# Ready-made byte addresses for the moving windows of a counting stage on one Trainium2 core

## The chip, the cores and the metric

One core of a Trainium2 chip runs the whole program. The metric is the device time of one execution in microseconds (us); the kernel before takes 1166.79 us (median of 3 runs, 1166.59 to 1166.88). PE is the matrix engine and PEld its weight load, DVE the vector engine, ACT the scalar engine, POOL the GpSimd engine, SP the engine that issues DMAs. Each engine has a sequencer, which reads the instructions in order, runs register and load instructions itself and hands the others to the engine.

## The reference, cut to what matters

The reference is a network of four graph layers on 3125 nodes and 100,000 edges, whose `dst` is sorted. The layers are an attention layer, a layer with an edge softmax over each destination, a summing layer, and one with three Chebyshev filters. The sums over edges have one form:

```
def _segment_sum(src, seg, n): return jax.ops.segment_sum(src, seg, n)
h_e = jax.ops.segment_sum(h[src], dst, num_segments=h.shape[0])      # layer 3
def prop(h): return segment_sum(wn[:, None] * h[row], col, n)          # layer 4
```

The kernel doesn't gather rows per edge. Its first stage, the count stage, builds a dense table `CT[source, destination]`: how many edges run from each source to each destination. All later sums over edges are matrix products with `CT`. This stage is the one that the change touches.

## The kernel before, in words

**The stages.** The program is one block with a stream of instructions per engine. `build_*` is the count stage, then come `proj_*`, `attn_*`, `prop_*` and `last_*`; between the first stages stands a meeting (`meet`, L71) at which all five engines wait for each other. The count stage ends at its first meeting, at about 360 us.

**How edges become counts.** The sorted edges are cut into chunks of 128. An item is one chunk against one window of four destinations (W = 4). Five items (GI = 5) that follow each other along the destinations make a group, four groups make a set (20 items), and six sets make a block of 120. There are 313 groups in 80 sets, and 14 blocks. Even groups walk the first half of the items, odd groups the second half, so group g and group g-2 touch neighbouring or equal places of `CT`, and g and g-1 do not.

**Per block.** POOL fetches the block's edges with two indirect DMAs (`gather`, L202 and L205) and makes keys of them (`keys`, L212 to L224). DVE splits the source number (`high`, L444 and L447), TensorE turns the keys (`turn_items`, L520 and L522), and ACT copies them out (`keep_items`, L576).

**Per set, on DVE.** Two large comparisons (both L435) make one-hot matrices: `oneS`, 128 edges by 20 items by 128 low source digits, and `mov`, 128 edges by 20 items by 100 columns (25 high source digits by 4 destinations). Each has two buffers (DEEP = 2). DVE may write the buffer of set s once TensorE has finished set s-2 (semaphore `counted`). Between the sets DVE runs the pieces of the edge softmax in an order written out by hand (`SOFT_AT`), and small jobs (`high`, `passes`, `slots`, `table`).

**Per set, on TensorE.** `load_windows` (L478 to L490) waits for the table and reads the set's 20 words from SBUF into registers: one TENSOR_LOAD, L485. Then come four groups. A group is five matmuls of 100 columns into one PSUM bank (L551), each shifted by its window's start, and one matmul with the identity (L555) that adds what `CT` holds at the group's place, 500 columns. Before L555 the stream waits until group g-2 has been placed back (semaphore `placed`). ACT waits for `counted` and writes the 500 sums into `CT` (L589), which adds one to `placed`.

**Where the addresses come from.** TensorE computes the first destination of each window into PSUM (`windows`, L513): a group's first word holds the start, the other four the distance from it (matrix `turnW`). DVE converts them to whole numbers in `wI` (`table`, L414), in item order. A table word is thus an offset in elements. `bass.ds(value, n)` turns it into an address: a register instruction (FUSED_REGOPS in the trace) multiplies the word by the element size and adds the base address. There is one before each of the 1252 shifted matmuls of L551 (the first of a group isn't shifted), one before each of the 313 matmuls of L555, and one before each of the 313 placements of L589. Where a semaphore wait stands before such an instruction, it is carried out on the register instruction: that of `placed` on the one of L555, that of `counted` on the one of L589. ACT reads every fifth word of the set, four in all.

Of the kernel before, what the change touches and what calls it, by code (L numbers as in the profile page):

```python
# [4 lines left out]
F32 = mybir.dt.float32  # L5
# [4 lines left out]
ALU = mybir.AluOpType  # L10
# [12 lines left out]
W = 4  # L23
WS = 2
LH = 795
NW = NP // W
# [22 lines left out]
class Kern:  # L49
# [15 lines left out]
    def sb(self, st, name, shape, dt):  # L65
        return st.enter_context(self.nc.sbuf_tensor(name, shape, dt))
# [34 lines left out]
GI = 5  # L101
SETS = 80
SET = 4 * GI
BLOCK = 6 * SET
# [16 lines left out]
             25: (4, 1)}  # L121


def before(g):

    return sum(1 for p in PRESENT if p < g)


def alloc_build(K, st):
    sb = K.sb  # L130
    K.iotaM = sb(st, "iotaM", [128, 25 * W], I16)
    K.iotaX = sb(st, "iotaX", [128, 128], I16)

    K.KL = sb(st, "KL", [128, RING, 2, BLOCK, 2], I16)
    K.GS = sb(st, "GS", [128, 2, CH], I32)
    K.GD = sb(st, "GD", [128, 2, CH], I32)
    K.dl = sb(st, "dl", [128, CH], F32)
    K.over = sb(st, "over", [128, CH], F32)
    K.under = sb(st, "under", [128, CH], F32)
    K.hi = sb(st, "hi", [128, 2, CH], I32)  # L140
    K.key = sb(st, "key", [128, CH], F32)
    K.va = sb(st, "va", [128, CH], F32)
    K.lo = sb(st, "lo", [128, 2, CH], F32)
    K.wI = [sb(st, "wI%d" % h, [b - a, BLOCK], I32) for h, (a, b) in enumerate(PARTS)]
    K.turnW = sb(st, "turnW", [BLOCK, BLOCK], F32)
    K.win = sb(st, "win", [BLOCK, NJ], F32)
    K.cI = sb(st, "cI", [BLOCK, NJ], I32)
    K.i4 = sb(st, "i4", [BLOCK, NJ], F32)
    K.jI = sb(st, "jI", [BLOCK, NJ], I32)
    K.row0 = sb(st, "row0", [1, BLOCK], F32)  # L150
    K.col0 = sb(st, "col0", [BLOCK, 1], F32)
    K.zf = sb(st, "zf", [128, 1], F32)
    K.onef = sb(st, "onef", [1, 1], F32)
    K.oneh = sb(st, "oneh", [128, 1], F16)
    K.lw = sb(st, "lw", [128, 7], I32)
    K.le = sb(st, "le", [128, 7], F32)
    K.cc = sb(st, "cc", [128, 7], I32)
    K.oneS = sb(st, "oneS", [128, DEEP, SET, 128], F16)
    K.mov = sb(st, "mov", [128, DEEP, SET, 25 * W], F16)
    K.cs = sb(st, "cs", [128, 4], F32)  # L160

    with ExitStack() as st2:
        K.iotaS = sb(st2, "iotaS", [128, SLOTS], I16)
        K.past = sb(st2, "past", [128, 7, 7 * BLOCK], F16)
    K.wv = sb(st, "wv", [128, J], F32)
    K.sp = sb(st, "sp", [128, J], BF16)
    K.sn = sb(st, "sn", [128, J], BF16)
    K.A1 = sb(st, "A1", [128, J], F32)
    K.A2 = sb(st, "A2", [128, J], F32)
    K.A3 = sb(st, "A3", [128, J], F32)  # L170
    K.ie = sb(st, "ie", [128, J], BF16)
    K.rows = sb(st, "rows", [1, 400], F32)
    K.CTf = K.CT[:, :, :].rearrange("p a d -> p (a d)").bitcast(F32)
# [196 lines left out]
def build_vector(v, K):  # L370
# [2 lines left out]
    v.memset(K.lw[:, 6:7], 32000).then_inc(S("lw_set"), 1)  # L373
    v.memset(K.zf[:, :], 0.0).then_inc(S("zf"), 1)
    v.memset(K.onef[:, :], 1.0)
    v.memset(K.oneh[:, :], 1.0).then_inc(step, own.up())


# [31 lines left out]

    def table(h):

        v.wait_ge(S("windows"), h + 1)
        v.tensor_copy(K.wI[h][:, :], K.bank(4)[0:PARTS[h][1] - PARTS[h][0], 128:128 + BLOCK]).then_inc(S("reg_set"), 1)  # L414

    for t in range(7):
        passes(0, t)
    v.wait_ge(S("identf"), 1)
    ident = K.identf[0:BLOCK, 0:BLOCK]
    v.tensor_copy(K.turnW[:, :], ident).then_inc(step, own.up())  # L420
    first = ident[:, 0:BLOCK:GI].unsqueeze(2).to_broadcast([BLOCK, BLOCK // GI, GI - 1])
    v.wait_ge(step, own.n)
    v.tensor_tensor(K.turnW[:, :].rearrange("p (m k) -> p m k", k=GI)[:, :, 1:GI],
                    ident.rearrange("p (m k) -> p m k", k=GI)[:, :, 1:GI], first, ALU.subtract).then_inc(step, own.up())
    slots(0)
    v.wait_ge(S("iota"), 6)
    v.wait_ge(S("passed"), 1)
# [48 lines left out]
    v.wait_ge(step, own.n)  # L476


def load_windows(K, e, ety, s, every):

    j, o = s // 6, SET * (s % 6)
    h = 0 if j == 0 else 1 if j < PARTS[2][0] else 2
    r = j - PARTS[h][0]
    e.wait_ge(K.S("reg_set"), h + 1)
    _, vals = K.nc.values_load_multi_w_load_instructions(  # L485
        K.wI[h][r:r + 1, o:o + SET:every], engines=[ety], min_val=0, max_val=W * (NW - 3),
        skip_runtime_bounds_check_because="a window's first destination by the staircase")
    n = SET // 4 // every
    return [[x if k == 0 else x.with_bounds(min_val=0, max_val=(GI - 1) * W) for k, x in enumerate(vals[n * r:n * r + n])]
            for r in range(4)]  # L490


def build_tensor(t, K):
    S, bank = K.S, K.bank
    t.wait_ge(K.own["v"].sem, K.row0_at)
    t.matmul(bank(5)[0:BLOCK, 0:1], K.row0[:, :], K.onef[:, :], start=True, stop=True).then_inc(S("item0"), 1)

    def sums(h):
        a, b = PARTS[h]
        for j in range(a, b):  # L500
            for t_ in range(7):
                if j == a:
                    t.wait_ge(S("past"), 7 * h + t_ + 1)
                m = t.matmul(bank(4)[0:BLOCK, j:j + 1], K.past[:, t_, BLOCK * (j - a):BLOCK * (j - a + 1)], K.oneh[:, :],
                             start=(t_ == 0), stop=(t_ == 6))
        m.then_inc(S("passed"), 1)

    def windows(h):
        a, b = PARTS[h]
        t.wait_ge(S("slot_w"), h + 1)  # L510
        if h:
            t.wait_ge(S("reg_set"), h)
        t.matmul(bank(4)[0:b - a, 128:128 + BLOCK], K.win[:, a:b], K.turnW[:, :], start=True, stop=True  # L513
                 ).then_inc(S("windows"), 1)

    def turn_items(j):
        t.wait_ge(S("key"), j + 1)
        if j:
            t.wait_ge(S("items"), j)
        t.transpose(bank(6)[:, 0:BLOCK], K.va[0:BLOCK, :], K.identf[0:BLOCK, 0:BLOCK])  # L520
        t.wait_ge(S("lo"), j + 1)
        t.transpose(bank(6)[:, BLOCK:2 * BLOCK], K.lo[0:BLOCK, j % 2, :], K.identf[0:BLOCK, 0:BLOCK]  # L522
                    ).then_inc(S("key_turned"), 1)

    def soft_turn(n, back):
        t.wait_ge(S("scan_v"), 2 * n + back + 1)
        if not back:
            t.transpose(bank(7)[0:1, 0:128], K.cs[:, 0:1], K.identf[:, :])
            t.transpose(bank(7)[0:1, 128:256], K.cs[:, 1:2], K.identf[:, :]).then_inc(S("scan_p"), 1)
        else:  # L530
            src = K.rows[:, 257:385] if n in (1, 3) else K.rows[:, 256:384]
            t.transpose(bank(7)[:, 256:257], src, K.identf[0:1, 0:1]).then_inc(S("scan_p"), 1)

    sums(0)
    windows(0)
    sums(1)
    turn_items(0)
    windows(1)
    t.wait_ge(S("identb"), 1)
    t.wait_ge(S("zero"), 5)  # L540
    for g in PRESENT:
        s, o = g // 4, GI * (g % 4)
        if g % 4 == 0:
            words = vals = to = None
            words = load_windows(K, t, mybir.EngineType.PE, s, 1)
            t.wait_ge(S("one_hot"), s + 1)
        vals = words[g % 4]
        ps = bank(g % 4)[:, 0:25 * GI * W].rearrange("p (a c) -> p a c", a=25)
        for k in range(GI):
            to = ps[:, :, 0:W] if k == 0 else ps[:, :, bass.ds(vals[k], W)]  # L550
            t.matmul(to, K.oneS[:, s % DEEP, o + k, :], K.mov[:, s % DEEP, o + k, :].rearrange("p (a w) -> p a w", a=25),  # L551
                     start=(k == 0), stop=False, skip_group_check=True)
        if g >= 2:
            t.wait_ge(S("placed"), INDEX[g - 2] + 1)
        t.matmul(ps, K.identb[:, :], K.CT[:, :, bass.ds(vals[0], GI * W)], start=False, stop=True, skip_group_check=True  # L555
                 ).then_inc(S("counted"), 1)
        if g == PRESENT[-1] or g // 4 != PRESENT[INDEX[g] + 1] // 4:
            if s == SUM_AT:
                sums(2)
            if s == SLOTS_AT:  # L560
                windows(2)
            if s in TURN_AT:
                turn_items(TURN_AT[s])
            if SOFT_AT.get(s) in SOFT_TURN:
                soft_turn(*SOFT_TURN[SOFT_AT[s]])
    t.wait_ge(S("counted"), len(PRESENT))


def build_scalar(a, K):
    S = K.S  # L570
# [13 lines left out]
    for i, g in enumerate(PRESENT):  # L584
        s = g // 4
        if g % 4 == 0:
            words = load_windows(K, a, mybir.EngineType.Activation, s, GI)
        a.wait_ge(S("counted"), i + 1)
        a.activation(K.CT[:, :, bass.ds(words[g % 4][0], GI * W)],  # L589
                     K.bank(g % 4)[:, 0:25 * GI * W].rearrange("p (a c) -> p a c", a=25), ACT.Copy).then_inc(S("placed"), 1)  # L590
        if g == PRESENT[-1] or s != PRESENT[i + 1] // 4:
            if s in TURN_AT:
# [1458 lines left out]
```

## Time and profile before

| | |
|---|---|
| median of 3 runs | 1166.79 us |
| span of the profiled execution, first to last instruction | 1161.5 us |
| what lies around the span, against that median | 5.3 us |
| busy share of the span: PE, DVE, ACT, POOL | 86%, 75%, 52%, 42% |
| mean granted TensorE clock over the span | 0.934 |
| the count stage | 0 to 360 us |

The profile is of one execution of its own; no separate time is given for it, so its span and the median are set side by side. Times in the trace are microseconds from the first instruction, durations are nanoseconds where it says so. A row of a group of instructions gives the line in the kernel, engine, operation, output<-input, count, busy time, the mean of one, and the engine's idle time before them with what ended it. "issue" means that nothing which the profile shows ended the wait: the sequencer itself was late. Register instructions and loads into registers belong to the sequencer; they are not counted as busy and carry the mark "q" behind the engine.

### The profile page before, as it was taken

The page shows a single profiled execution, that of the slowest core. Times are in us where ns is not written, and L with a number is a line of the kernel's source. Part 1 is how long each engine was busy: PE and PEld are TensorE (multiplying, and loading weights), DVE is VectorE, ACT ScalarE, POOL GpSimd, SP SyncE. Part 2 cuts the span into 40 slices and gives each one's busy share as a digit, 9 for nine tenths or more (in the row PEclk, how much of TensorE's full clock was granted, in tenths as well). Part 3 has the DMA queues.
Part 4 walks back from the last instruction along what each step waited for, and adds up shares of the span by engine and source line. Part 5 has one row for each costly group of instructions (what it writes and reads, how often), then busy time and mean ns, then how long its engine had stood idle before and what let it go on. Part 6 is the DMA issues. An engine that isn't in the chain of part 4 may idle for free.

```text
span 1161.5 us, 23065 instructions
## 1 busy us (share of the span) xinstructions
PE 1003.2 (86%) x8302; PEld 612.5 (53%) x8302; DVE 876.5 (75%) x1318; ACT 608.1 (52%) x824; POOL 492.1 (42%) x522
## 2 busy tenths in 40 slices
PE   3887777777778779999999999996999699999995
PEld 2554455554544423223223333333669599999984
DVE  8668888888765569999999999997846654543366
ACT  7455556565563579898989898881100000001132
POOL 8434443343310069999999999980000000000000
PEclk9788999896897979999999999997999799999997
DMA  0010000000001631222222223221001100010111
GB/s 9 25 44 8 10 6 5 6 5 8 17 1 50 202 82 44 62 50 63 48 59 51 64 58 72 51 65 48 1 1 42 42 25 24 2 35 11 57 45 42
DMA packets 98715, 44.63 MB, mean 38 GB/s; under 512 B 85006, under 2 KB 96526, under 8 KB 98482
## 3 DMA queue, kind: packets, MB, share of 16 engines
q1 hardware_dynamic: 96914, 41.43, 13.4%
q0 software_dynamic: 1696, 1.74, 0.6%
q8 instruction: 73, 1.20, 0.4%
q14 instruction: 32, 0.26, 0.1%
HBM read 30.58 MB, written 12.56 MB: 37 GB/s over the span
## 4 chain that ended last, share of the span: by engine, by line
PE 77%; issue 9%; DVE 7%; ACT 3%; DMA 1%; POOL 1%; SPq 1%; DVEq 0%; ACTq 0%; POOLq 0%
PE PS L1298 18%; PE PS L1062 12%; PE PS L551 11%; PE PS L1072 11%; PE PS L555 8%; PE PS L1306 3%; PE PS L1773 3%; PE PS L1051 3%; ACT Eb L1114 2%; PE PS L1289 1%; POOL Eb L975 1%; DVE Eb L1134 1%; PE PS L875 1%; DMA kd<-QH 1%; PE PS L1759 1%
## 5 line engine op out<-in xcount | busy, mean ns | idle before, releaser
L1114 ACT ACTIVATE Eb<-PS,small 128x1024 f32<-128x1024 f32 (+4 forms) x350 | 333.3, 1003 | 45.0 <-PE PS L1062 40.3
L1134 DVE TENSOR_TENSOR Eb<-Eb,PS 128x2048 f32<-128x2048 f32 (+4 forms) x175 | 341.8, 2011 | 18.8 <-POOL Eb L975 10.1
L975 POOL TENSOR_SCALAR Eb<-Eb 128x1024 f32<-128x1024 f32 (+4 forms) x350 | 318.9, 935 | 76.7 <-ACT Eb L1114 73.2
L589 ACT ACTIVATE CT<-PS 128x500 f32 x313 | 183.7, 587 | 142.5 <-PE PS L555 134.3
L551 PE MATMUL PS<-mov,oneS 128*128 128x100 f16 x1565 | 183.3, 228 | 78.8 <-issue 74.7
L551 PEld LDWEIGHTS PS<-mov,oneS 128*128 128x128 f16 x1565 | 145.4, 105 | 158.4 <-issue 112.6
L1298 PE MATMUL PS<-hs,CT 128*128 128x192 f16 (+1 forms) x2500 | 213.3, 247 | 3.6 <-DVE SG L1539 1.6
L1298 PEld LDWEIGHTS PS<-hs,CT 128*128 128x128 f16 (+1 forms) x2500 | 207.9, 99 | 7.3 <-DVE SG L1539 2.3
L1062 PE MATMUL PS<-Qb,Kb 96*128 96x512 f16 (+3 forms) x700 | 180.4, 362 | 13.7 <-DMA Kb<-kd 10.8
L435 DVE TENSOR_TENSOR oneS<-iotaX,KL 128x2560 f16<-128x2560 int16 x80 | 120.4, 1505 | 70.3 <-PE PS L555 67.8
L1072 PE MATMUL PS<-Eb,V 128*25 128x512 f32 (+3 forms) x1400 | 166.7, 548 | 0.8 <-DVE Eb L1134 0.8
L1062 PEld LDWEIGHTS PS<-Qb,Kb 96*128 96x128 f16 (+1 forms) x700 | 42.3, 98 | 198.6 <-ACT Eb L1114 184.4
L555 PE MATMUL PS<-CT,identb 128*128 x313 | 139.1, 444 | 1.0 <-ACT CT L589 0.8
L1739 POOL MEMSET CT<- 1x384 f32 x1 | 0.4, 416 | 305.9 <-PE PS L1298 305.9
L435 DVE TENSOR_TENSOR mov<-iotaM,KL 128x2000 f16<-128x2000 int16 x80 | 98.7, 1234 | 0.0
L217 POOL TENSOR_SCALAR key<-hi 120x128 f32<-120x128 int32 x14 | 8.8, 628 | 172.9 <-DVE hi L444 172.9
L1419 ACT ACTIVATE hs<-PS 96x96 f32<-96x96 f32 x9 | 2.2, 247 | 138.2 <-PE PS L1330 138.2
L1051 PEld LDWEIGHTS PS<-identb,CT 128*128 128x128 f16 (+1 forms) x625 | 49.5, 98 | 44.0 <-DVE Eb L1134 7.8
L1051 PE MATMUL PS<-identb,CT 128*128 128x128 f16 (+1 forms) x625 | 66.5, 220 | 4.4 <-DVE Eb L1134 4.4
L1539 DVE TENSOR_REDUCE SG<-PS 128x96 f32<-128x192 f32 (+1 forms) x75 | 24.8, 352 | 60.1 <-PE PS L1298 59.8
L1773 PE MATMUL PS<-hs,CT 97*128 97x297 f32 (+1 forms) x200 | 42.8, 357 | 0.3 <-ACT CT L1820 0.3
L1306 PE MATMUL PS<-CT,identb 128*128 128x500 f16 (+1 forms) x157 | 38.2, 400 | 3.3 <-SPq L71 3.3
(281 smaller groups left out, 905.9 us busy)
## 6 DMA issues: line engine op xcount, KB each, us to landing
Kb<-kd SPq DMA_DIRECT2D x168, 96.0 KB, 2.3
qd<-QH SPq DMA_DIRECT2D x12, 192.0 KB, 2.7
kd<-QH SPq DMA_DIRECT2D x12, 192.0 KB, 3.1
hs<-t_d SPq DMA_DIRECT2D x12, 192.0 KB, 2.5
Qb<-qd SPq DMA_DIRECT2D x4, 384.0 KB, 3.8
CT<-x_d SPq DMA_DIRECT2D x1, 1200.0 KB, 7.1
x_d<-B SPq DMA_DIRECT2D x6, 192.0 KB, 1.9
t_d<-A SPq DMA_DIRECT2D x6, 192.0 KB, 1.8
```

The source lines that it names most:

```text
L435: return v.tensor_tensor(out.rearrange("p e (c two) -> p e c two", two=2), v_in, k_in, ALU.is_equal)
L551: t.matmul(to, K.oneS[:, s % DEEP, o + k, :], K.mov[:, s % DEEP, o + k, :].rearrange("p (a w) -> p a w", a=25), start=(k == 0), stop=False ...
L555: t.matmul(ps, K.identb[:, :], K.CT[:, :, bass.ds(vals[0], GI * W)], start=False, stop=True, skip_group_check=True).then_inc(S("counted"), 1)
L589: a.activation(K.CT[:, :, bass.ds(words[g % 4][0], GI * W)], K.bank(g % 4)[:, 0:25 * GI * W].rearrange("p (a c) -> p a c", a=25), ACT.Copy ...
L975: g.tensor_scalar(e, e, EHI, ELO, ALU.min, ALU.max).then_inc(S("clamped"), 1)
L1051: m = p.transpose(K.cntv[it % 2][0:r, 128 * i:128 * i + w], K.CT[0:w, B0[b] + i, 128 * t:128 * t + r], K.identb[0:w, 0:w])
L1062: m = p.matmul(bank(h)[0:r, 0:wb], K.Kb[:, it % NK, h, 0:r], K.Qb[:, b % 2, h, 0:wb], start=True, stop=True)
L1072: m = p.matmul(bank(4)[32 * h:32 * h + 25, 0:wb], K.V[0:r, t, h, :], K.Eb[0:r, it % NE_, h, 0:wb], start=(t == 0), stop=(t == NT - 1), til ...
L1114: a.activation(e, ps, ACT.Exp, scale=K.unsc[0:r, :]).then_inc(S("score_exp"), 1)
L1134: v.tensor_tensor(e, e, cn, ALU.mult).then_inc(S("weighed"), 1)
L1298: m = p.matmul(bank(t % FIRST)[0:r, 0:w], K.CT[:, a, 128 * t:128 * t + r], hs[:, a, :, :].rearrange("p k d -> p (k d)"), start=(a == 0), s ...
L1773: m = p.matmul(ps[:, c:297], K.TT[0:r, s, 128 * k:128 * k + 128], K.GC[0:r, k, c:297], start=(k == 0), stop=(k == 3), skip_group_check=True)
```

## The change

- The table holds byte addresses. Its 20 words of a set are in a new order: first the starts of the four groups, as addresses in `CT`, then four times four addresses in the PSUM bank of the group. `turnW` is scaled so that the products are bytes (by 2 for `CT`, by 4 for PSUM); `table` adds the base address of `CT` with one instruction and the banks' addresses (`bankA`, set by four memsets) with another.
- The expressions in `load_windows` take the base off again and divide by the element size, so that the address that the program asks for is the loaded word itself, with no register instruction in between.
- With no register instruction before L555 and L589, the waits for `placed` and `counted` stand on the matmul and on the placement.
- ACT reads four words that are neighbours, where it read every fifth of twenty. TensorE still reads twenty.

```
+    K.bankA = sb(st, "bankA", [7, 4], F32)
+    K.ct_at = K.nc.lookup_mloc(K.CT).addr
+    for q in range(4):
+        v.memset(K.bankA[:, q:q + 1], float(PSUM_AT + BANK_BYTES * q))
...
     def table(h):
+        n = PARTS[h][1] - PARTS[h][0]
         v.wait_ge(S("windows"), h + 1)
-        v.tensor_copy(K.wI[h][:, :], K.bank(4)[0:PARTS[h][1] - PARTS[h][0], 128:128 + BLOCK]).then_inc(S("reg_set"), 1)
+        ps = K.bank(4)[0:n, 128:128 + BLOCK].rearrange("r (s q k) -> r s q k", q=4, k=GI)
+        words = K.wI[h][:, :].rearrange("r (s w) -> r s w", w=SET)
+        v.tensor_scalar(words[:, :, 0:4], ps[:, :, :, 0], float(K.ct_at), None, ALU.add).then_inc(step, own.up())
+        banks = K.bankA[0:n, :].unsqueeze(1).unsqueeze(3).to_broadcast([n, BLOCK // SET, 4, GI - 1])
+        v.tensor_tensor(words[:, :, 4:SET].rearrange("r s (q k) -> r s q k", q=4), ps[:, :, :, 1:GI], banks, ALU.add
+                        ).then_inc(S("reg_set"), 1)
...
-    v.tensor_copy(K.turnW[:, :], ident).then_inc(step, own.up())
+    v.tensor_scalar(K.turnW[:, :], ident, 2.0, None, ALU.mult).then_inc(step, own.up())
...
+    v.wait_ge(step, own.n)
+    rest = K.turnW[:, :].rearrange("p (m k) -> p m k", k=GI)[:, :, 1:GI]
+    v.tensor_scalar(rest, rest, 4.0, None, ALU.mult).then_inc(step, own.up())
...
-def load_windows(K, e, ety, s, every):
+def load_windows(K, e, ety, s, rest):
...
     _, vals = K.nc.values_load_multi_w_load_instructions(
-        K.wI[h][r:r + 1, o:o + SET:every], engines=[ety], min_val=0, max_val=W * (NW - 3),
+        K.wI[h][r:r + 1, o:o + (SET if rest else 4)], engines=[ety], min_val=K.ct_at, max_val=PSUM_AT + 4 * BANK_BYTES,
...
+    starts = [(x.with_bounds(min_val=K.ct_at, max_val=top, guaranteed_mod_val=0, out_of_modulus=2) - K.ct_at) // 2
+              for x in vals[0:4]]
+    inside = [[(x.with_bounds(min_val=PSUM_AT + BANK_BYTES * q, max_val=PSUM_AT + BANK_BYTES * q + 4 * REL_MAX,
+                              guaranteed_mod_val=0, out_of_modulus=4) - PSUM_AT) // 4
+               for x in vals[4 + (GI - 1) * q:4 + (GI - 1) * (q + 1)]] for q in range(4 if rest else 0)]
...
-            to = ps[:, :, 0:W] if k == 0 else ps[:, :, bass.ds(vals[k], W)]
+            to = ps[:, :, 0:W] if k == 0 else bass.AP(K.PS, inside[g % 4][k - 1], [[4096, 128], [GI * W, 25], [1, W]])
...
-        t.matmul(ps, K.identb[:, :], K.CT[:, :, bass.ds(vals[0], GI * W)], start=False, stop=True, skip_group_check=True
+        t.matmul(ps, K.identb[:, :], K.CT[:, :, bass.ds(starts[g % 4], GI * W)], start=False, stop=True, skip_group_check=True
...
-        a.activation(K.CT[:, :, bass.ds(words[g % 4][0], GI * W)],
+        a.activation(K.CT[:, :, bass.ds(starts[g % 4], GI * W)],
```

## Rows read from the trace of the kernel before

**Rows 1.** The page's costliest groups, lines of the count stage.

```profile
L589 ACT ACTIVATE CT<-PS 128x500 f32 x313 | 183.7, 587 | 142.5 <-PE PS L555 134.3
L551 PE MATMUL PS<-mov,oneS 128*128 128x100 f16 x1565 | 183.3, 228 | 78.8 <-issue 74.7
L435 DVE TENSOR_TENSOR oneS<-iotaX,KL 128x2560 f16<-128x2560 int16 x80 | 120.4, 1505 | 70.3 <-PE PS L555 67.8
L435 DVE TENSOR_TENSOR mov<-iotaM,KL 128x2000 f16<-128x2000 int16 x80 | 98.7, 1234 | 0.0
```

**Rows 2.** Busy time of each engine from the first one-hot to the stage's end.

```profile
core 0: us, PE busy (x) PEld busy (x) DVE busy (x) ACT busy (x) POOL busy (x), PEclk, DMA share, GB/s
22.50:360.00 337.50, 256.78 (x1965) 166.11 (x1965) 262.86 (x249) 194.95 (x328) 128.11 (x117) 0.87 0.04 12
```

**Rows 3.** Timeline of PE over one set: start us, us, instructions, idle before.

```profile
202.02 0.68 PE L551 MATMUL PS<-mov,oneS 128*128 128x100 f16 x5 [1.06 <-issue]
202.60 0.39 PE L555 MATMUL PS<-CT,identb 128*128 x1
203.26 0.39 PE L555 MATMUL PS<-CT,identb 128*128 x1
...
204.52 0.39 PE L555 MATMUL PS<-CT,identb 128*128 x1
```

**Rows 4.** Sequencer instructions by source line, whole trace: min/median/max ns.

```profile
L485 PEldq TENSOR_LOAD <-wI x80: 1355/1359/1549, 29.3 to 356.7; - x80
L551 PEldq FUSED_REGOPS  x1252: 37/46/51, 30.9 to 358.5; - x179
L555 PEldq FUSED_REGOPS  x313: 37/42/42, 31.4 to 358.6; - x157
```

**Rows 5.** Timelines of ACT and DVE over the same set.

```profile
203.10 2.50 ACT L589 ACTIVATE CT<-PS 128x500 f32 x4 [1.43 <-PE PS L555]
201.07 1.49 DVE L435 TENSOR_TENSOR oneS<-iotaX,KL 128x2560 f16<-128x2560 int16 x1 [1.59 <-PE PS L555]
202.48 1.19 DVE L435 TENSOR_TENSOR mov<-iotaM,KL 128x2000 f16<-128x2000 int16 x1
```

**Rows 6.** Who waited for whom, 22.5 to 360 us: total us, times, longest.

```profile
POOL key L217 <- DVE hi L444: 172.9, 13, 18.2
DVE oneS L435 <- PE PS L555: 67.8, 56, 4.6
```

**Rows 7.** Timeline of PEld around the L555 matmul that starts at 202.60 us.

```profile
202.59 0.10 PEld L555 LDWEIGHTS PS<-CT,identb 128*128 128x128 f16 x1
202.61 0.10 PEld L551 LDWEIGHTS PS<-mov,oneS 128*128 128x128 f16 x1
```

**Rows 8.** Back-to-back 500-column matmuls at full clock, and five-matmul groups at half clock.

```profile
849.66 2.76 PE L1306 MATMUL PS<-CT,identb 128*128 128x500 f16 x12
...
47.92 0.62 PE L555 MATMUL PS<-CT,identb 128*128 x1
48.33 0.62 PE L551 MATMUL PS<-mov,oneS 128*128 128x100 f16 x5
48.76 0.62 PE L555 MATMUL PS<-CT,identb 128*128 x1
```

**Rows 9.** Third load of table words, and PE's timeline around it.

```profile
L485 PEldq TENSOR_LOAD <-wI x1: 1358/1358/1358, 44.9 to 44.9; - x1
...
42.54 4.31 PE L504 MATMUL PS<-oneh,past 128*120 128x1 f16 x42
```

**Rows 10.** DVE: the long wait near the start, the table, and `turnW`.

```profile
50.31 1.49 DVE L435 TENSOR_TENSOR oneS<-iotaX,KL 128x2560 f16<-128x2560 int16 x1 [4.60 <-PE PS L555]
L414 DVE CAST wI<-PS x3: 208/262/264, 22.4 to 61.2; 1x120 int32<-1x120 f32 x1, 7x120 int32<-7x120 f32 x1, 6x120 int32<-6x120 f32 x1
9.82 0.26 DVE L423 TENSOR_TENSOR turnW<-identf 120x96 f32<-120x96 f32 x1
```

More of the change, by code:

```diff
@@ L121 @@
              25: (4, 1)}
+PSUM_AT = 0x2000000
+BANK_BYTES = 2048
+REL_MAX = (GI - 1) * W
 def before(g):
@@ L484, in load_windows @@
     e.wait_ge(K.S("reg_set"), h + 1)
+    top = K.ct_at + 2 * W * (NW - 3)
     _, vals = K.nc.values_load_multi_w_load_instructions(
-        K.wI[h][r:r + 1, o:o + SET:every], engines=[ety], min_val=0, max_val=W * (NW - 3),
[L487 to L490, printed above, removed]
+        K.wI[h][r:r + 1, o:o + (SET if rest else 4)], engines=[ety], min_val=K.ct_at, max_val=PSUM_AT + 4 * BANK_BYTES,
+        skip_runtime_bounds_check_because="addresses made from a window's first destination by the staircase")
+    starts = [(x.with_bounds(min_val=K.ct_at, max_val=top, guaranteed_mod_val=0, out_of_modulus=2) - K.ct_at) // 2
[3 more added lines that the diff above has]
+               for x in vals[4 + (GI - 1) * q:4 + (GI - 1) * (q + 1)]] for q in range(4 if rest else 0)]
+    return starts, inside
 def build_tensor(t, K):
@@ L543, in build_tensor @@
         if g % 4 == 0:
-            words = vals = to = None
-            words = load_windows(K, t, mybir.EngineType.PE, s, 1)
+            starts = inside = to = None
+            starts, inside = load_windows(K, t, mybir.EngineType.PE, s, True)
             t.wait_ge(S("one_hot"), s + 1)
-        vals = words[g % 4]
         ps = bank(g % 4)[:, 0:25 * GI * W].rearrange("p (a c) -> p a c", a=25)
         for k in range(GI):
-            to = ps[:, :, 0:W] if k == 0 else ps[:, :, bass.ds(vals[k], W)]
+            to = ps[:, :, 0:W] if k == 0 else bass.AP(K.PS, inside[g % 4][k - 1], [[4096, 128], [GI * W, 25], [1, W]])
             t.matmul(to, K.oneS[:, s % DEEP, o + k, :], K.mov[:, s % DEEP, o + k, :].rearrange("p (a w) -> p a w", a=25),
@@ L586, in build_scalar @@
         if g % 4 == 0:
-            words = load_windows(K, a, mybir.EngineType.Activation, s, GI)
+            starts, _ = load_windows(K, a, mybir.EngineType.Activation, s, False)
         a.wait_ge(S("counted"), i + 1)
-        a.activation(K.CT[:, :, bass.ds(words[g % 4][0], GI * W)],
+        a.activation(K.CT[:, :, bass.ds(starts[g % 4], GI * W)],
                      K.bank(g % 4)[:, 0:25 * GI * W].rearrange("p (a c) -> p a c", a=25), ACT.Copy).then_inc(S("placed"), 1)
```

## The prediction

> **What bounds the kernel now.** I read the page's groups first [rows 1]. In the count stage DVE's two one-hot builds and ACT's placements wait for PE's L555, and PE's L551 waits for "issue", 74.7 us in all: the stage's pace comes from PE's sequencer. The window over the stage [rows 2] shows no engine full in its 337.5 us: DVE 262.9, PE 256.8 by modelled ends, ACT 195.0. The timeline of one set [rows 3] splits that. PE's L555 matmuls start at 202.60 and 203.26, and the fourth at 204.52, so a group takes (204.52 - 202.60) / 3 = 0.64 us. The array needs less: twelve 500-column matmuls back to back take 2.76 us, thus about 0.22 each, and at half clock five matmuls of 100 columns take 48.33 - 47.92 = 0.41 us including their share of the next [rows 8], so 0.21 at full clock. That makes 0.43 us a group. What fills 0.64 is the sequencer. By source line [rows 4], each shifted matmul has a register instruction of 46 ns median; the group shows 0.64 / 5 = 0.13 us for a register instruction, a weight load and a matmul. Then, once a set, the sequencer loads 20 words in 1.36 us [rows 4]. In this set nothing covers that: PE stood idle for 1.06 us before its next L551 at 202.02 [rows 3]. From the first L551 at 202.02 over the fourth L555 at 204.52 and the load to the next first L551 it is 2.50 + 1.36 + 0.05 = 3.9 us; 337.5 / 80 = 4.2 us with the start and the stretches at half clock. I take 4.05 for a set.
>
> **The change, part by part.**
>
> *Register instructions.* 1252 + 313 go from PE's sequencer, at 46 and 42 ns: 57.6 + 13.1 = 71 us of register work, and more with what stands around each. ACT loses 313. What is left to issue is a weight load and a matmul, and these come close together: the weight load of L555 at 202.59, its matmul (whose address is already in a register) at 202.60 [rows 3], the next weight load at 202.61 [rows 7]. So I cost a pair at 0.01 to 0.02 us, 24 pairs a set at 0.4 us. The other bound is that a register-addressed matmul without its register instruction costs what the whole step costs now, 0.13 us; no row speaks for that, the 0.01 us between neighbours speaks against it.
>
> *The waits move.* Today `placed` is waited for on the register instruction, so the sequencer stands there until ACT has placed group g-2 and only then goes on to the next group and to the table load. With the wait on the matmul the sequencer can hand it over and read on. What is queued behind the waiting instruction: the next group's five matmuls, which write another bank and need nothing of ACT, and then the next set's load. That a load runs while matmuls are still outstanding is shown once: the third TENSOR_LOAD starts at 44.9 us, while L504's 42 matmuls run from 42.54 to 46.85 [rows 9]; at 4.31 / 42 = 0.10 us each that leaves about 18 of them to come. So the sequencer may lead by some 17 matmuls, most of a set of 24, and a load of 1.36 us then hides behind the last three groups. The Trainium skill (Advanced Engine Details and Errata, Engine Queue Depths) gives TensorE a queue of 64 instructions, ScalarE 8. By it the lead would be 32 pairs, a whole set and more; by the row it is about 17 pairs; the load hides by either. No row shows a register-addressed matmul that itself carries a wait; that is the open point, bounded by 0 (it queues like others) and by the load's whole 1.36 us a set (the sequencer stands as before).
>
> *ACT.* Its placements run at 2.50 / 4 = 0.63 us [rows 5], 587 ns of it work [rows 1]. The round from L555 over ACT back to L555 of g+2 is 0.39 (matmul) + 0.11 (its end 202.99 to ACT's 203.10) + 0.59 + about 0.1 = 1.2 us for two groups, 0.6 a group. So on a set with full buffers PE and ACT need 4 x 0.61 = 2.44 us. ACT's four neighbouring words in place of four strided ones are at most its load, which its sequencer can now do ahead; I cost it at nothing, with ACT idle for 142.5 us as cover.
>
> *DVE becomes the bound.* A set's one-hots take from 201.07 to 203.67, 2.60 us [rows 5], over 2.44. Added up with the softmax pieces and the small jobs DVE has 262.9 us of work [rows 2]; it doesn't shrink. Of its idle 74.6 us, 67.8 are waits for PE's L555 [rows 6]. I keep 5 us of them: the longest, 4.60 us at 50.31 [rows 10], comes from the 42 matmuls of L504, which stay. After the last one-hot one group has to be counted and placed: 0.2 + 0.4 + 0.6 = 1.2 us, say 1.4.
>
> *What is added.* DVE gets one more table instruction for each of three tables and one more for `turnW`, 0.26 us each [rows 10], 1.0 us together on an engine that is now the bound; the four memsets lie in its wait for POOL at the start. The bounds are 0.3 us (only `turnW` late) and 2 us.
>
> *The clock.* The granted clock of the stage is 0.87 on average [rows 2]. It has two levels, 1.2 and 2.4 GHz, so about 26% of the stage, 88 us or some 21 sets, is at half. There a group is array-bound at 48.76 - 47.92 = 0.84 us [rows 8], a set 3.35. Today that hides under 4.05; against a DVE set of 2.60 it costs 0.75 us. With the softmax pieces a set of DVE is 262.9 / 80 = 3.3 on average, and about two thirds of the sets are well under that: 21 x 0.67 x 0.75 = 10.5 us if the share stays. PE will do the same matmuls in less time, with shorter pauses, so I expect fewer falls and take half, 5 us; bounds 0 and, with the whole stage at half clock, 80 x 3.35 = 268 plus some 30 us for the long softmax sets, 298, less the 269 us (262.9 + 5 + 1.4) without it: 29 us.
>
> **Sum.** 262.9 + 5 + 1.4 + 1.0 + 5 = 275.3 us in place of 337.5: 62 us less. The span goes from 1161.5 to 1099.3. The stages behind begin at a meeting of all engines, so they move forward as they are; the softmax's last output is written well before. The median of the runs shown stands 5.3 us above the profiled span (1166.8), so the time is 1104.6, rounded to 1105 us.
>
> **The rivals.**
>
> *A: a matmul with a register address and a wait still holds the sequencer.* The register instructions are gone, but the load stays exposed. From the last L555 of a set to the next set's first it is 1.36 + 0.05 + 0.25 (five matmuls) = 1.66; from first to fourth 0.43 + 1.2 = 1.6. A set is 3.3 us at full clock, more than DVE's on most sets and 3.7 at half. About 80 x 3.35 + 25 for long softmax sets = 293 + 4: 40 us less, 1127 us. For it: every such wait sits on a register instruction today. Against it: waits on plain matmuls don't hold the sequencer.
>
> *B: the half clock holds for the whole stage.* By the bound above the stage takes 269 + 1 + 29 = 299 us, 38 us less: 1128 us. Against it: a set would then be dense, and in dense stretches the clock is near full (0.934 over the span).
>
> *C: the register instructions don't go.* If taking the base off and adding it back isn't folded, the same count stays, the waits with them; the stage keeps 4.05 us a set and pays about 1 us for the tables: 1168 us, no change that can be told.
>
> *D, slower: POOL becomes the bound.* POOL's busy time is 128.1 us for 14 blocks [rows 2], 9.2 us each, and it waits for DVE's `hi` for 172.9 us, 13 us a block [rows 6]. A block would last 6 x 3.3 = 20 us in place of 24. If DVE's denser work slowed POOL's key chain (fetch, compare, key, turn) to more than today's 24.3 us a block, 2.6 times its busy time, PE would wait in `turn_items`, and at 25 us the stage would be 13 x 0.7 = 9 us longer: 1176 us. The wait of 172.9 us speaks against it.
>
> **How the numbers follow.** Forecast 0.62, A 0.14, B 0.08, C 0.06, D 0.05, and 0.05 for a result between forecast and none. The forecast's own range is 1095 (no half clock, no added idle: 263 + 4) to 1115 (all of today's half clock, and the two buffers emptying now and then). The range reaches over A: 1095 to 1130. A measurement of this kernel tells about 0.2%, 2.3 us, from no change. Faster 0.88 (forecast, A, B and most between), same 0.06 (C), slower 0.06 (D and a rest).
>
> **What would show it.** No FUSED_REGOPS on PE or ACT (else C). DVE's idle time before `oneS` falls from 70.3 us to about 10, and PE's idle time before L551 has DVE's `mov` as its releaser, not "issue" (if "issue" stays, with 1 us a set, it is A). The table load of a set starts while that set's L555 are still to come. The stage ends near 298 us instead of 360. The clock of the stage is above 0.87 (under 0.6 is B). POOL's wait for `hi` shrinks from 172.9 to about 115 us (13 blocks, 4.3 us shorter each), and stays well over nothing (else D). The prediction is wrong if sets whose DVE work is 2.60 us follow each other at more than 3 us with the clock at full.

## The result, and the profile after

The changed kernel takes 1108.45 us (median of 4 runs, 1108.01 to 1110.53) against 1166.84 us before on the same chip: a ratio of 0.9503, 95% interval 0.9489 to 0.9517, so 58 us less. The prediction was 1105 us. The page of the profile after begins with the span, and its groups answer to [rows 1]:

```profile
span 1106.3 us, 21195 instructions
L610 ACT ACTIVATE CT<-PS 128x500 f32 x313 | 167.8, 585 | 101.3 <-PE PS L576 101.0
L572 PE MATMUL PS<-mov,oneS 128*128 128x100 f16 x1565 | 124.2, 210 | 97.2 <-DVE mov L453 53.6
L453 DVE TENSOR_TENSOR oneS<-iotaX,KL 128x2560 f16<-128x2560 int16 x80 | 120.7, 1509 | 11.8 <-PE PS L576 9.8
L453 DVE TENSOR_TENSOR mov<-iotaM,KL 128x2000 f16<-128x2000 int16 x80 | 100.6, 1258 | 0.0
```

(L551, L555, L589 and L435 of before are L572, L576, L610 and L453 now.) 1870 instructions fewer than the 23065 of before: that is the 1565 + 313 register instructions, less the eight that DVE got. DVE's idle time before `oneS` fell from 70.3 to 11.8 us, and what PE waits for before its five matmuls is now DVE's `mov` for 53.6 of 97.2 us by the profile and "issue" for 43.6, where it was nearly all "issue". The window over the count stage, which answers to [rows 2], has the same columns:

```profile
22.50:303.10 280.60, 180.39 (x1965) 114.88 (x1965) 263.85 (x253) 179.28 (x328) 168.44 (x117) 0.98 0.05 14
```

The stage ends at 303.1 us instead of 360.0, 56.9 us earlier; DVE's work in it is the same (263.9 against 262.9 us) and now fills 94% of it. Behind the stage little changed: from its end to the span's end it is 803.2 us, before 801.5. The clock of the stage rose from 0.87 to 0.98. POOL got busier, 168.4 against 128.1 us with the same 117 instructions: its operations take longer (L227, L220 of before, 2036 ns on average against 763). That this comes from a DVE that works beside them more often is my reading; no run shows it alone.

The timeline of one set (start us, us, engine, instructions, idle before) answers to [rows 3]:

```profile
244.68 0.39 PE L572 MATMUL PS<-mov,oneS 128*128 128x100 f16 x5 [1.02 <-issue]
...
244.91 0.38 PE L576 MATMUL PS<-CT,identb 128*128 x1
...
245.12 0.39 PE L572 MATMUL PS<-mov,oneS 128*128 128x100 f16 x5
...
245.35 0.38 PE L576 MATMUL PS<-CT,identb 128*128 x1
...
245.96 0.10 PEld L576 LDWEIGHTS PS<-CT,identb 128*128 128x128 f16 x1 [0.16 <-ACT CT L610]
245.96 0.39 PE L576 MATMUL PS<-CT,identb 128*128 x1
...
246.44 0.39 PE L576 MATMUL PS<-CT,identb 128*128 x1
...
247.85 0.25 PE L572 MATMUL PS<-mov,oneS 128*128 128x100 f16 x2 [0.87 <-DVE mov L453]
```

The four L576 start at 244.91, 245.35, 245.96 and 246.44. From the first to the second it is 0.44 us, the array's own time; the third and fourth wait for ACT (in the trace the wait is carried out on L576's weight load). That is 1.53 us in place of 1.92. But the next set's first matmul comes only at 247.85, 1.41 us behind the fourth. The sequencer's rows of that stretch say why:

```profile
L504 PEldq TENSOR_LOAD <-wI x1: 1359/1359/1359, 246.4 to 246.4; - x1
L504 ACTq TENSOR_LOAD <-wI x1: 307/307/307, 246.9 to 246.9; - x1
```

PE's load of 20 words starts together with the fourth L576, not ahead of it, and its 1.36 us stand open as before. (The timeline names `mov` as what ended the wait; `mov` was done at 247.46 and the load at 247.80.) It is so in nearly all sets. Of the 79 loads behind the first none starts less than 0.046 us behind the placement that the last L576 waits for, and three quarters start at most 0.051 us behind it; in 61 sets the next first matmul comes within 0.1 us of the load's end, so the load was what ended last there. The lengths of the sets, from first matmul to first matmul, agree: their median is 3.18 us, and 42 of 79 are 3.16 to 3.18; before the median was 4.07.

### The profile page after: what moved, and what is told of

Read it like the earlier page. It is cut to its first block, busy times and chain, and to the rows that moved or that the text cites. A ratio compares the mean times of both kernels' runs of the same rounds, so it can differ in the third digit from the quotient of the medians.

```text
span 1106.3 us, 21195 instructions
## 1 busy us (share of the span) xinstructions
PE 927.6 (84%) x8302; PEld 562.0 (51%) x8302; DVE 877.7 (79%) x1326; ACT 592.4 (54%) x824; POOL 532.7 (48%) x522
## 4 chain that ended last, share of the span: by engine, by line
PE 64%; DVE 18%; issue 7%; ACT 3%; DMA 3%; SPq 3%; POOL 1%; DVEq 0%; ACTq 0%
PE PS L1319 19%; PE PS L1083 13%; PE PS L1093 12%; DVE oneS L453 6%; DVE mov L453 4%; PE PS L1327 3%; PE PS L1794 3%; PE PS L1072 3%; PE PS L572 2%; PE PS L576 2%; ACT Eb L1135 2%; PE PS L1310 2%; SPq L266 1%; POOL Eb L996 1%; DVE Eb L1155 1%
## 5 line engine op out<-in xcount | busy, mean ns | idle before, releaser
L610 ACT ACTIVATE CT<-PS 128x500 f32 x313 | 167.8, 585 | 101.3 <-PE PS L576 101.0
L572 PE MATMUL PS<-mov,oneS 128*128 128x100 f16 x1565 | 124.2, 210 | 97.2 <-DVE mov L453 53.6
L572 PEld LDWEIGHTS PS<-mov,oneS 128*128 128x128 f16 x1565 | 98.9, 99 | 147.7 <-DVE mov L453 67.4
L453 DVE TENSOR_TENSOR oneS<-iotaX,KL 128x2560 f16<-128x2560 int16 x80 | 120.7, 1509 | 11.8 <-PE PS L576 9.8
L576 PE MATMUL PS<-CT,identb 128*128 x313 | 123.6, 395 | 1.9 <-ACT CT L610 0.9
L453 DVE TENSOR_TENSOR mov<-iotaM,KL 128x2000 f16<-128x2000 int16 x80 | 100.6, 1258 | 0.0
L224 POOL TENSOR_SCALAR key<-hi 120x128 f32<-120x128 int32 x14 | 8.7, 623 | 83.9 <-DVE hi L462 83.7
```

The source lines that it names most:

```text
L453: return v.tensor_tensor(out.rearrange("p e (c two) -> p e c two", two=2), v_in, k_in, ALU.is_equal)
L576: t.matmul(ps, K.identb[:, :], K.CT[:, :, bass.ds(starts[g % 4], GI * W)], start=False, stop=True, skip_group_check=True).then_inc(S("coun ...
L610: a.activation(K.CT[:, :, bass.ds(starts[g % 4], GI * W)], K.bank(g % 4)[:, 0:25 * GI * W].rearrange("p (a c) -> p a c", a=25), ACT.Copy). ...
```

## The experiments

All ran against the kernel before on the same chip. The short diffs are against the changed kernel; where a kernel has lines more, the line numbers of its rows shift. "Stage end" is the end of the last placement of the profiled run.

**e1, a wait as an instruction of its own.** The edit adds a wait for `zero`, which is long reached. It was meant to turn the wait for `placed` into an instruction of PE's sequencer, with the idle one on the matmul. The trace shows the reverse: the new instruction waits for `zero`, and the wait for `placed` stays on L576 (L577 here).

```
         if g >= 2:
             t.wait_ge(S("placed"), INDEX[g - 2] + 1)
+            t.wait_ge(S("zero"), 5)
```

> The changed kernel with the wait for placed as an instruction of its own before L576, so that PE's sequencer certainly stands there. Theory H (the sequencer stands at L576 in the changed kernel anyway, because the load of the next set's words starts at 246.44 us together with the last L576 at 246.44): 1108 to 1113 us, sets still 3.17 to 3.25 us. Theory Q (as predicted: the waiting matmul is queued, the sequencer reads on, and that is worth about 20 us): 1125 to 1135 us.

Measured: 1110.86 us, ratio 0.9513 (0.9493 to 0.9534), median set 3.18 us, stage end 305.9 us. As the wait for `placed` wasn't moved, this time doesn't decide between H and Q, the prediction's theory. The rows do:

```profile
L576 PEldq EVENT_SEMAPHORE  x311: 51/51/51, 31.2 to 304.7; - x156
...
249.04 0.10 PEld L577 LDWEIGHTS PS<-CT,identb 128*128 128x128 f16 x1 [0.16 <-ACT CT L611]
```

The new instruction is the sequencer's own, so its start tells how far the sequencer has read. In the set of the second row the third group's L577 waits for ACT until 249.04, and the new instruction of the fourth group, five matmuls further on, starts at 249.05. Of 310 such pairs none has it start less than 0.06 us behind the placement for which the L577 ahead of it waits. So the sequencer does stand at a waiting instruction, as H says. Where nothing is open it runs ahead: earlier in the set three new instructions start at 247.782, 247.908 and 248.034 us, and in the 0.126 us between two of them, 0.051 of it their own, it issues six weight loads with their matmuls, 0.0125 us each.

**e2, the 1252 register instructions back.** The table holds half of each PSUM address, so each has to be doubled.

```
-        v.memset(K.bankA[:, q:q + 1], float(PSUM_AT + BANK_BYTES * q))
+        v.memset(K.bankA[:, q:q + 1], float((PSUM_AT + BANK_BYTES * q) // 2))
...
-    v.tensor_scalar(rest, rest, 4.0, None, ALU.mult).then_inc(step, own.up())
+    v.tensor_scalar(rest, rest, 2.0, None, ALU.mult).then_inc(step, own.up())
...
-                              guaranteed_mod_val=0, out_of_modulus=4) - PSUM_AT) // 4
+                              guaranteed_mod_val=0, out_of_modulus=2) - PSUM_AT // 2) // 2
```

> The changed kernel with a register instruction back before each of the 1252 shifted matmuls (the table holds half the address, so it has to be doubled); the waits stay on the matmul. If these instructions are the gain: a group 0.6 us, a set 3.8 to 3.95 us, 1150 to 1160 us. If the waits' register instructions are the gain: 1108 to 1115 us.

Measured: 1174.03 us, ratio 1.0051 (1.003 to 1.0071), median set 4.23 us. The whole gain is gone, and the time is above the 1160 us that I had as the upper end. The rows by source line and of the timeline say why:

```profile
L572 PEldq FUSED_REGOPS  x1252: 81/85/99, 31.1 to 365.5; - x179
...
  issue: 175.4, 248
...
202.89 0.38 PE L576 MATMUL PS<-CT,identb 128*128 x1
203.11 0.60 PE L572 MATMUL PS<-mov,oneS 128*128 128x100 f16 x5
203.54 0.38 PE L576 MATMUL PS<-CT,identb 128*128 x1
```

This kernel's register instruction takes 85 ns where that of before took 46 [rows 4]; four of them with their surroundings fill the 0.65 us from one L576 to the next, as five shorter ones did. So e2 prices the step too high, by an estimate of 16 x 0.04 = 0.6 of the 1.05 us that it adds to a set. It shows that register instructions between the matmuls set a group's pace, and not what the 1252 cost at 46 ns: by the same estimate 0.4 us a set, of the 0.9 us that the change took off (4.07 to 3.18).

**e3, the other 313 on PE and 313 on ACT back, with the waits on them.** The table holds half of the `CT` addresses.

```
-        v.tensor_scalar(words[:, :, 0:4], ps[:, :, :, 0], float(K.ct_at), None, ALU.add).then_inc(step, own.up())
+        v.tensor_scalar(words[:, :, 0:4], ps[:, :, :, 0], float(K.ct_at // 2), None, ALU.add).then_inc(step, own.up())
...
-    starts = [(x.with_bounds(min_val=K.ct_at, max_val=top, guaranteed_mod_val=0, out_of_modulus=2) - K.ct_at) // 2
+    starts = [x.with_bounds(min_val=K.ct_at // 2, max_val=top) - K.ct_at // 2
```

> The changed kernel with a register instruction back before each L576 on PE and each L610 on ACT, with the wait on it. Theory H: the sequencer stood there anyway, so only the instruction's own 0.09 us on each side of the round is added: a set 3.3 to 3.4 us, 1113 to 1120 us. Theory Q: the sequencer is held again, 1125 to 1135 us.

```profile
L576 PEldq FUSED_REGOPS  x313: 46/46/46, 31.1 to 310.6; - x157
```

Measured: 1119.09 us, ratio 0.9582 (0.9557 to 0.9606), median set 3.38 us. That is 0.8% or 9 us above the changed kernel, in theory H's range and 6 us under Q's: the register instructions lie in the round from L576 over ACT to L576 of g+2, and a set has one and a half such rounds. In this kernel the waits stand on register instructions again, as before, so the move of the waits is worth 9 us at most, the instructions' own time included. These 0.2 us a set and e2's 0.4 leave some 0.3 us to both kinds together; no run separates that.

**e4, the wait on the first of the five matmuls,** which has a fixed address.

```
+        if g >= 2:
+            t.wait_ge(S("placed"), INDEX[g - 2] + 1)
         for k in range(GI):
...
-        if g >= 2:
-            t.wait_ge(S("placed"), INDEX[g - 2] + 1)
```

> The changed kernel with the wait for placed on the first of a group's five matmuls (its address is fixed, no register) in place of L576. Theory R (only a waiting instruction with a register address holds the sequencer): the load of the next words starts more than 0.5 us ahead of the set's last L576, 1100 to 1106 us. Theory W (any waiting instruction holds back the load): it starts 0.2 to 0.3 us ahead of the last L576, together with the waiting matmul, 1108 to 1116 us.

Measured: 1120.88 us, ratio 0.9592 (0.9564 to 0.962), median set 3.31 us; as theory W says, but 5 us above its range. (A set's first matmul waits for `one_hot` already; there the wait for `placed` becomes an instruction of its own, 79 in all.) The load's place is what the run was for. PE's timeline of a set's end, and the load by source line (two in that window, the second is this one):

```profile
247.80 0.38 PE L576 MATMUL PS<-CT,identb 128*128 x1
248.04 0.40 PE L574 MATMUL PS<-mov,oneS 128*128 128x100 f16 x5
248.28 0.38 PE L576 MATMUL PS<-CT,identb 128*128 x1
...
L504 PEldq TENSOR_LOAD <-wI x2: 1358/1360/1362, 244.8 to 248.0; - x2
```

The load starts with the waiting matmul at 248.04, 0.24 us ahead of the last L576 (median over all sets 0.23). So it isn't the register address: a load into registers starts when the last instruction ahead of it that waits has been released, with a fixed address or one from a register. [Rows 9] (the load is the fourth, not the third) doesn't contradict it: of the 42 matmuls there only the first seven wait for a semaphore, and the 17 still to start at 44.93 us only stood in line.

**e5, the load in pieces of four words between the groups.** `load_part` reads four words. Each group's four shifted addresses are loaded one group ahead, behind the five matmuls and before L576; a set's four starts at the end of the set before.

```
+        at = starts[q]
+        if g != PRESENT[-1]:
+            if q == 3:
+                starts = load_part(K, s + 1, -1)
...
+            inside = load_part(K, n // 4, n % 4)
         if g >= 2:
             t.wait_ge(S("placed"), INDEX[g - 2] + 1)
```

> The changed kernel with PE's load of 20 words cut into pieces of four (ScalarE's load of four neighbours takes 0.31 us), each issued one group ahead: behind a group's five matmuls and before its L576; at a set's end two of them. Theory H (the load is exposed because it is issued behind a waiting matmul, with nothing left in the queue): the pieces hide behind the array's 0.43 us a group and the wait for ScalarE, sets fall to DVE's 2.6 us where DVE has no other work, stage 9 to 12 us shorter, 1096 to 1101 us, DVE's idle before oneS under 6 us. Rival D (DVE with 263.9 of 280.6 us busy is the bound already): 1106 to 1109 us.

Measured: 1105.95 us, ratio 0.9484 (0.9468 to 0.95), stage end 301.1 us, a quarter of the sets at 2.77 us or less. PE's waits for "issue" before its five matmuls fall from 43.6 to 6.9 us, so the load is hidden, but the stage is only 2 us shorter where 9 to 12 were expected. The time is 2 us less by the ratios, whose intervals overlap, and 4.6 us less than e7's on the same chip; it lies at rival D's range and not at H's. The rows show what is left:

```profile
L504 PEldq TENSOR_LOAD <-wI x393: 325/329/518, 29.5 to 297.8; - x197
...
22.50:301.10 278.60, 207.21 (x1965) 124.99 (x1965) 264.15 (x253) 187.01 (x328) 172.73 (x117) 0.92 0.05 14
...
DVE sp L312 <- DMA wv<-in_edge_weight: 4.4, 1, 4.4
```

DVE works 264.2 of 278.6 us. And it now comes 4.4 us too early to the first softmax piece, whose six DMAs are sent at a fixed place. SP issues them from 47.8 to 71.9 us, with 15 us on one of them, and the last one, which DVE waits for, has landed at 84.4.

**e6, the same pieces at the set's start,** where the load of 20 words stood.

> The same five pieces of four words, all at the set's start, where the load of 20 words stands: the place alone against the size alone. Theory H: 5 x 0.31 = 1.53 us in place of 1.36, so sets of 3.34 in place of 3.17 us, 1112 to 1118 us. Rival: if splitting helps by itself, under 1106 us.

Measured: 1140.37 us, ratio 0.9787 (0.9756 to 0.9817), sets of 3.70 us. That is 22 us above H's range, in its direction. A piece takes 0.33 us (ACT's 0.31 was my measure), and from one piece's start to the next's it is 0.39, so five cost 0.5 to 0.6 us more than one load of 20. The set grows by 0.53 us, all of it: what the sequencer spends at the set's start is paid in full. It is e5's place that helps, not the splitting.

**e7, ACT reads all 20 words.**

> The changed kernel with ScalarE reading all 20 words (1.36 us in place of 0.31). Its load starts with the set's last placement and the next placement is due 1.6 us later, so it stays hidden: 1107 to 1110 us. Rival: ScalarE's shorter load is part of the gain: 1.05 us more on the sets of 3.17 us, over 1120 us.

Measured: 1110.57 us, ratio 0.9521 (0.9503 to 0.954), sets 3.17 us. ACT's load takes 1.26 us instead of 0.31 and costs nothing that can be told. So the four neighbouring words on ACT, the last part of the change, are no part of the gain.

**e8, the whole load ahead of the last L576.**

> The changed kernel with the next set's load of 20 words moved ahead of the last group's L576. Theory H: it starts when the third L576's wait is over, some 0.45 us earlier, and overlaps 0.4 us of array work; sets of about 2.9 us, 1099 to 1104 us. Rival: the last L576 comes 0.9 us late, ScalarE's placements with it, and nothing is won: 1107 us or more.

Measured: 1115.95 us, ratio 0.9575 (0.9559 to 0.9591), stage end 308.8 us, median set 3.21 us. A quarter of the sets are as short as H said, 2.96 us or less, and still the rival was right on the time: the load now keeps the last L576 waiting, which starts 1.42 us behind the load's start, and with it ACT's placement and DVE, which waits 16.7 us for L576 in place of 9.8. So the 0.4 us of array work that it overlaps doesn't pay. A load of 1.36 us fits between no two groups of 0.44 to 0.6 us; pieces of 0.33 us do.

**e9, e5 with the softmax starting three sets later,** and the changed kernel again beside it.

```
-SOFT_AT = {16 + sum(SOFT_GAPS[:k]): k for k in range(len(SOFT_GAPS))}
+SOFT_AT = {19 + sum(SOFT_GAPS[:k]): k for k in range(len(SOFT_GAPS))}
```

> e5 with the softmax pieces starting three sets later (19 in place of 16), because in e5 DVE waits 4.4 us at 80 us for the edges' DMA, where the changed kernel waits 1.5 us. If that wait is given back: 1101 to 1104 us. Rival: DVE's work is the bound and the wait was cover for PE's backlog: 1105 to 1107 us.

> The changed kernel as it is, on the same chip as e9: 1107 to 1111 us. e9 is faster by 4 to 7 us if both its steps hold, by 2 us or less if DVE alone decides.

Measured: e9 1102.32 us, ratio 0.9453 (0.9432 to 0.9475); the changed kernel 1110.73 us, ratio 0.9522 (0.95 to 0.9545). e9 is 8.4 us faster than the changed kernel on the same chip, more than the 4 to 7 expected, and the fastest kernel here that does all the work. The later softmax wasn't run without the pieces, so the shares of the two are known only from e5 on another chip. The wait for the DMA is gone from the list, and DVE's work fills 264.75 of 273.2 us:

```profile
22.50:295.70 273.20, 205.93 (x1965) 122.82 (x1965) 264.75 (x253) 186.50 (x328) 178.53 (x117) 0.93 0.05 14
```

**e10 and e11, DVE made lighter,** on the changed kernel and on e5. The softmax pieces work on 64 of 782 columns, so most of that work is left out; the reciprocal is an addition.

```
+    J = 64
...
-    wv, sp, sn, A1, A2, A3, ie, cs, rows = K.wv, K.sp, K.sn, K.A1, K.A2, K.A3, K.ie, K.cs, K.rows
...
+    wv, sp, sn, A1, A2, A3, ie = (t[:, 0:J] for t in (K.wv, K.sp, K.sn, K.A1, K.A2, K.A3, K.ie))
+    cs, rows = K.cs, K.rows
...
-    v.reciprocal(A1[:, :], A2[:, :]).then_inc(step, own.up())
+    v.tensor_scalar(A1[:, :], A2[:, :], 1.0, None, ALU.add).then_inc(step, own.up())
```

> The changed kernel with DVE's softmax pieces over 64 of 782 columns (most of that work is left out, about 45 us of DVE time, and the reciprocal is an addition). Theory B (two bounds: PE's sets of 3.17 us with the exposed load, and DVE's work where it is more): the stage falls only to 80 x 3.2 + 30 = 286 us, 15 to 18 us less, 1090 to 1095 us. Theory D (DVE alone is the bound): 40 us less or more, 1070 us.

> The same lightening on e5, where PE's load is in pieces between the groups. Theory B: the load's floor is gone, sets of 2.6 to 2.9 us, the stage ends at 257 to 265 us, 1062 to 1070 us, some 25 us under e10. Theory D: no difference to e10 beyond 3 us.

Measured: e10 1092.53 us, ratio 0.9367 (0.9338 to 0.9396); e11 1079.59 us, ratio 0.9256 (0.9227 to 0.9285). The waits and the windows over the stage, first of e10, then of e11:

```profile
PE PS L574 <- issue: 70.6, 67, 7.6
DVE oneS L455 <- PE PS L578: 21.0, 40, 3.2
...
22.50:288.30 265.80, 178.98 (x1965) 114.48 (x1965) 237.20 (x253) 179.08 (x328) 164.72 (x117) 0.99 0.05 15
```

```profile
PE PS L592 <- DVE mov L455: 26.2, 39, 4.7
...
22.50:273.90 251.40, 199.50 (x1965) 119.44 (x1965) 236.64 (x253) 186.07 (x328) 173.62 (x117) 0.97 0.05 16
```

DVE became lighter by 27 us, not by the 45 that I had written, which is enough to explain why e11 is 10 us above its range. e10 answers the question: with 27 us less for DVE the stage is only 14.8 us shorter, nearly all sets are 3.17 us long (3.29 every sixth, where the keys are turned), and PE waits for "issue" more, 70.6 us against 43.6. With the pieces between the groups (e11) the same lightening gives 27.2 us: the stage follows DVE's work one to one. So theory B holds: the changed kernel has two bounds, the load's floor of 3.17 us a set and DVE's work where that is more, and they lie close together.

## Why the prediction was right, point by point

The time came out within 4 us of the forecast, but one link of its mechanism failed, and by the sign that the prediction itself had set: light sets follow each other at 3.17 us, more than 3, with the stage's clock at 0.98. That the number still fits is in part luck. From the 1104.6 us of the sum, the stage adds 5.3 and the time behind it 1.7, and what lies around the span takes 3.2 off, which makes 1108.4; within the stage the open load and the clock term err in opposite directions.

- *The sequencer sets the pace before.* Right: in e2 register instructions before the shifted matmuls alone bring a group back to 0.65 us, though they are longer ones than those of before.
- *A pair of weight load and matmul with a ready address costs 0.01 to 0.02 us to issue.* Right: 0.0125 us by the rows of e1, and from the first L576 to the second it is 0.44 us, the 0.43 that I had for the array.
- *The waits move, the sequencer reads on, the load hides.* Wrong. This is the step that failed. The row behind it [rows 9] showed a load beside queued matmuls, but none of those still to start waited for a semaphore. The changed kernel and e4 show that a load stands behind any waiting matmul, and e3 that the move of the waits is worth 9 us at most. With a lead of 17 matmuls the load would have started during the second group, and it starts with the fourth L576, its 1.36 us open. The Trainium skill ("Advanced Engine Details and Errata", Engine Queue Depths) gives TensorE a queue of 64 instructions. That depth doesn't describe this trace either: the load doesn't start ahead of the waiting L576. The sentence against rival A, that waits on plain matmuls don't hold the sequencer, had no row, and e4 shows the opposite. Rival A was thus right on the mechanism, for waiting matmuls with a fixed address as for those with one from a register.
- *Rival A's price.* It was too high, 3.35 us a set and 25 us on top for the softmax sets. The floor is 3.17 us, and the terms don't add: where DVE's work makes a set long, the load hides behind it. So A's mechanism gives about the forecast's time, which nobody had foreseen: luck.
- *DVE becomes the bound.* Right for the sum and not for each set. Its work, 262.9 + 1.0, came out at 263.85 us. I kept 5 us of idle time for it and 1.4 us behind it; with the open load it idles 16.8 us in the window. In e9 8.5 us of these are left.
- *The clock.* I took 5 us for half-clock stretches. The stage's granted clock rose to 0.98, so this term was near nothing. It cancels about half of the load's share.
- *The sum.* The stage was predicted at 275.3 us and took 280.6; the span was to fall by 62 us and fell by 55.2. The times fell by 58.4. The profiled execution of before was a quick one: in nearly all runs that have both, the time is 1.7 to 2.2 us above the span, and not the 5.3 that I had put around it.
- *What is added, ACT's words, POOL.* DVE's added instructions are within 1 us as costed. ACT's words cost and give nothing (e7). POOL waits 83.7 us for `hi` in place of 172.9; I had expected 115. It didn't become the bound, but it loses room from both sides: shorter blocks and 40 us more in its operations.
- *Not foreseen:* DVE arrives at the first softmax piece before its DMA has landed, 1.5 us in the changed kernel and 4.4 in e5.

What stays open: why the stage's clock is 0.92 in e5 and 0.93 in e9 and 0.98 in the changed kernel, with the same matmuls (no run varied it alone), how the gain splits between the 1252 and the 626 register instructions, and what the later softmax alone is worth.

## What to carry to other kernels

Where many small matmuls have addresses from registers, look at the sequencer's rows between them: a table that holds finished addresses takes 0.12 us a matmul off the sequencer for one more vector instruction a table. What that is worth depends on the next limit: here the array took over at 0.44 us a group, and a set of 20 windows became 0.9 us shorter, 0.045 us a window. A row that shows a load beside queued work shows nothing for queued work that waits; loads into registers belong in pieces between the matmuls, one group ahead. When the bound moves to an engine with a plan written out by hand, check what its first steps wait for.

## What the runs showed of the hardware

- A load into registers starts when the last waiting instruction ahead of it on its engine is released: never less than 0.046 us behind the placement that releases it in the changed kernel, and 0.24 us ahead of L576 in e4. Matmuls that only stand in line may still be outstanding, 17 of them in [rows 9].
- The load's time goes by the words and their spacing. On ACT four neighbouring words take 0.31 us, four at a distance of five words took 0.89 (median, before), twenty neighbours 1.26; on PE four take 0.33 and twenty 1.36. Pieces follow each other at 0.39 us.
- A weight load and its matmul take 0.0125 us of the sequencer (e1), with five of the six matmuls addressed from registers; it is the instruction that computes the address that costs, 46 ns busy and 0.12 us with its surroundings, or 85 ns and 0.16 in the form that e2 needs.
